# The first mixer's triangular inverse, merged in 32x32 tiles instead of full-width products

## Chip, cores and metric

One core of a Trainium2 chip runs the whole program. The metric is the device time of one execution in microseconds; three runs of the kernel before are shown.

## The reference, cut to what matters

The program is two layers of a sequence model on 2 x 2048 tokens of width 128: a gated delta-rule mixer, a two-deep windowed-attention block, a second (RWKV-like) mixer, another two-deep block, with norms between. Only the first mixer is touched. Per head (16 heads, keys of 64, values of 128) it is a recurrence over the tokens:

```
S = S * exp(g_t)
mem = k_t . S
delta = (v_t - mem) * b_t
S = S + k_t (x) delta
o_t = (q_t * scale) . S
```

The kernel does it in chunks of 128 tokens. Within a chunk the deltas solve a unit lower-triangular system per head: with A the decayed, scaled products of the chunk's keys, delta = (I + A)^-1 (v - decayed k.S), times beta. The change is in how (I + A)^-1 is built.

## The kernel before

The first mixer takes 32 chunks, one after the other (2 sequences of 16; a loop body of four chunks, run three times, and the last four written out). Sixteen heads go as four groups of four (`gi`), one PSUM bank a group. Every engine has its own order of work, written out by hand in its `body`; semaphores (`Signal`) tie them. While TensorE is in chunk n, the projections, decays and key products of chunks n + 1 and n + 2 are made ready between its steps.

The inverse has two parts. Ahead of the chunk, VectorE's `nA` (minus A, transposed; L824) is cut into its eight 16x16 diagonal blocks a head; they go through DRAM (`turn` on the DMA queue) so that VectorE's `inverse` works on all 128 blocks at once, and come back, transposed, as diagonal blocks of a zeroed `Tm`, [128, 16 heads, 128], which shares its buffer with `gV`. That landing is the signal `T_in`. Then `solve` on TensorE doubles the blocks three times (`LEVELS` 16, 32, 64). Before each level `turn_T` turns `Tm` (L496) and ScalarE copies it to `X` (L676). At a level, z = A times the even blocks (L512, for the last level L510), VectorE masks it into `Z` (L868), X times Z gives the block beside the diagonal (L521, last L519), and VectorE adds it to `Tm` (L876; last level: copies it into `X`, L873). Z keeps only the even blocks' 64 columns, but the weights, `X` or `Tm` and `nA`, are 128 rows by 128 columns, except in the last level. After it L531 applies `X` to the residues `R` (made by VectorE's `residues`, L860, from the state products L474), L537 and L543 make outputs and the new state.

Around it: `late` on ScalarE evicts the state's outputs (L671) before the first copy to `X`, and decays the state (L681) after the last. `X`'s buffer later holds squares and the turned output `yT`, read by L562, whose result VectorE takes in `tail`. POOL writes `gV` for the next chunk (`growth`, L984) once the last level's z is done, and zeroes `Tm` (L994) after masking the decays; `k_norms` (L977) runs in every second chunk. On VectorE the decays of the next chunk stand between the levels (`decays_first`, `decays_second`, L772 to L791).

## Time and profile before

| | |
|---|---|
| three runs, us | 5441.55, 5464.05, 5478.0 (median 5464.05) |
| profiled execution, span, us | 5452.6 |
| TensorE busy, us (share) | 4831.1 (89%) |
| VectorE busy, us (share) | 3836.5 (70%) |
| ScalarE busy, us (share) | 2736.9 (50%) |
| POOL busy, us (share) | 2285.8 (42%) |
| mean granted TensorE clock | 0.926 |

The span runs from the first to the last instruction of one execution; no time beside it was kept for that execution, so it stands among the three runs as one of its own. The engines overlap, so the shares don't add up. The granted clock is a share of 2.4 GHz. An fp32 matmul shows as two records, each with a weight load (PEld) and a product (PE); a turn shows as one.

### The profile page before, as it was taken

What the parts mean: (1) busy time and instruction counts of PE and PEld (TensorE: products, weight loads), DVE (VectorE), ACT (ScalarE), POOL (GpSimd) and SP (SyncE); (2) the same over time, 40 slices, a digit from 0 to 9 for tenths busy, and PEclk for the clock granted to TensorE, in tenths of its full rate; (3) what the DMA queues carried; (4) which work ended last, traced back from release to release, by engine and by line L of the source; (5) the groups of instructions that cost most, each with busy time, mean ns of one, the idle gap of its engine ahead of it and who ended that gap; (6) DMA issues with size and microseconds to landing.
All of it is one profiled execution on the core that took longest, in us unless ns stands there. A gap on an engine that the chain in (4) does not pass through costs nothing. (4 is left out here: it accounts for less than half of the span.)

```text
span 5452.6 us, 104905 instructions
## 1 busy us (share of the span) xinstructions
PE 4831.1 (89%) x36890; PEld 3535.1 (65%) x36890; DVE 3836.5 (70%) x9111; ACT 2736.9 (50%) x6711; POOL 2285.8 (42%) x1860
## 2 busy tenths in 40 slices
PE   5999999999999999999889989984488778998998
PEld 3787777877777787777766556641156665654665
DVE  4766667777677766767578668746699657866874
ACT  2444445444544544545478658724400116875882
POOL 2434334344334434434267347514322116743751
PEclk7999999999999999999999999986699758998998
DMA  2000000000000000000100000000000000000000
GB/s 86 5 9 7 7 9 7 7 9 7 7 9 10 5 9 8 6 9 9 34 1 0 25 5 0 0 7 0 8 1 1 1 1 30 0 24 5 0 0 16
DMA packets 170085, 52.60 MB, mean 10 GB/s; under 512 B 142304, under 2 KB 166112, under 8 KB 168928
## 3 DMA queue, kind: packets, MB, share of 16 engines
q1 hardware_dynamic: 168160, 44.30, 3.7%
q8 instruction: 232, 3.80, 0.3%
q10 hardware_dynamic: 1536, 3.21, 0.2%
q14 instruction: 157, 1.29, 0.1%
HBM read 36.99 MB, written 10.49 MB: 9 GB/s over the span
## 5 line engine op out<-in xcount | busy, mean ns | idle before, releaser
L799 DVE SCALAR_TENSOR_TENSOR gd_qkT<-gd_ps,gd_w_qk,gd_qkT 128x256 f32<-128x256 f32 x768 | 367.2, 482 | 193.3 <-ACT gd_qkT L632 172.7
L984 POOL TENSOR_TENSOR gd_gV<-gd_g,cst 128x512 f32<-128x512 f32 x128 | 130.3, 1040 | 860.1 <-PE gd_ps L510 860.1
L417 PE MATMUL gd_ps<-gd_taps,gd_xwins 128*128 128x512 f32 x1024 | 465.3, 597 | 0.0
L676 ACT ACTIVATE gd_X<-gd_ps 128x512 f32<-128x512 f32 x384 | 201.1, 620 | 452.9 <-PE gd_ps L496 452.6
L1540 ACT ACTIVATE L_ffn_s<-L_ffn_s,L_ffn_nb,L_ffn_r 128x128 f32<-128x128 f32 x1024 | 419.4, 482 | 3.1
L1360 POOL TENSOR_TENSOR L_ffn_t<-L_ffn_t 128x512 f32<-128x512 f32 x128 | 190.2, 1486 | 391.8 <-DVE L_ffn_t L1581 391.8
L417 PEld LDWEIGHTS gd_ps<-gd_taps,gd_xwins 128*128 128x128 f32 x1024 | 192.8, 191 | 191.1 <-issue 185.6
L868 DVE TENSOR_TENSOR gd_Z<-gd_ps,cst 128x256 f32<-128x256 f32 x384 | 162.7, 424 | 129.6 <-PE gd_ps L512 111.1
L1579 DVE TENSOR_TENSOR L_ffn_t<-L_ffn_ps,L_ffn_sb_rope 128x512 f32<-128x512 f32 x256 | 176.8, 691 | 101.8 <-PE L_ffn_ps L1385 101.8
L521 PE MATMUL gd_ps<-gd_Z,gd_X 128*128 128x64 f32 x2048 | 239.2, 275 | 0.0
L512 PE MATMUL gd_ps<-gd_gV,gd_nA 128*128 128x64 f32 x2048 | 237.9, 275 | 0.0
L512 PEld LDWEIGHTS gd_ps<-gd_gV,gd_nA 128*128 128x128 f32 x2048 | 236.3, 194 | 0.0
L521 PEld LDWEIGHTS gd_ps<-gd_Z,gd_X 128*128 128x128 f32 x2048 | 233.8, 192 | 0.0
L1428 PEld LDWEIGHTS L_ffn_ps<-L_ffn_kT,L_ffn_qT 64*64 64x64 f32 (+1 forms) x4096 | 148.5, 137 | 113.7 <-issue 98.2
L496 PE MATMUL gd_ps<-cst,gd_gV 128*128 128x128 f32 x1536 | 194.6, 280 | 31.0 <-DMA gd_gV<-gd_inverses 28.9
L860 DVE SCALAR_TENSOR_TENSOR gd_v<-gd_ps,gd_n_ec,gd_v 128x128 f32<-128x128 f32 x512 | 135.2, 342 | 123.0 <-PE gd_ps L474 120.8
L1362 POOL TENSOR_TENSOR L_ffn_r<-L_ffn_ss,L_ffn_mhalf 128x8 f32<-128x8 f32 x128 | 210.8, 1647 | 10.3 <-DVE L_ffn_ss L1603 5.1
L1029 POOL TENSOR_TENSOR gd_gate<-gd_gate,gd_o 128x512 f32<-128x512 f32 x128 | 159.5, 1277 | 126.3 <-DVE gd_o L885 126.3
L1369 POOL TENSOR_TENSOR L_ffn_r<-L_ffn_ss,L_ffn_mhalf 128x8 f32<-128x8 f32 x128 | 210.8, 1647 | 0.0
L990 POOL TENSOR_TENSOR gd_decay<-gd_decay,cst 128x512 f32<-128x512 f32 x128 | 186.7, 1490 | 47.1 <-ACT gd_decay L664 46.9
L687 ACT ACTIVATE gd_X<-gd_o 128x128 f32<-128x128 f32 x512 | 150.3, 295 | 106.0 <-DVE gd_o L885 106.0
L496 PEld LDWEIGHTS gd_ps<-cst,gd_gV 128*128 128x128 f32 x1536 | 175.3, 147 | 39.0 <-DMA gd_gV<-gd_inverses 32.2
(389 smaller groups left out, 13625.6 us busy)
## 6 DMA issues: line engine op xcount, KB each, us to landing
L_ffn_sb_rope<-in_rope SPq DMA_DIRECT2D x4, 2048.0 KB, 8.3
gd_tap_row<-in_L_attn_conv_v SPq DMA_DIRECT2D x2, 2048.0 KB, 15.6
gd_blocks<-gd_nA SPq DMA_DIRECT2D x256, 16.0 KB, 1.7
gd_Z<-gd_blocks SPq DMA_DIRECT2D x32, 128.0 KB, 2.0
gd_inverses<-gd_Z SPq DMA_DIRECT2D x32, 128.0 KB, 1.7
gd_gV<-gd_inverses SPq DMA_DIRECT2D x256, 16.0 KB, 1.9
L_ffn_sb_wqkv<-in_L_ffn_wqkv SPq DMA_DIRECT2D x4, 768.0 KB, 8.9
out<-out_tok SPq DMA_DIRECT2D x8, 256.0 KB, 2.6
```

Source lines behind the costliest of these rows:

```text
L417: ins = pe.matmul(ps[4 + i % 2][:], xwin(j)[:, t:t + P], taps[:, t, 512 * i:512 * (i + 1)], start=(t == 0), stop=(t == TAPS - 1))
L496: ins = pe.transpose(ps[4 + gi][:, P * k:P * (k + 1)], Tm[:, HG * gi + k], ident)
L512: ins = pe.matmul(ps[gi][:, 64 * k:64 * (k + 1)], nA[:, h], even(Tm, h, h + 1, s)[:, 0], start=True, stop=True)
L521: ins = pe.matmul(ps[gi][:, 64 * k:64 * (k + 1)], X[:, h], Z[:, h], start=True, stop=True)
L676: act.activation(heads(X, gi).rearrange("p h x -> p (h x)"), ps[4 + gi][:], ACT.Copy).then_inc(x_s.sem, 1)
L799: ins = dve.scalar_tensor_tensor(produced(j, i), ps[6 + i % 2][:, P + t:P + t + WIDE], w_tap[:, at, t:t + 1], produced(j, i), ALU.mult, AL ...
L990: pool.tensor_tensor(heads(decay, gi), heads(decay, gi), cst[:, C_UPTO:C_UPTO + P].unsqueeze(1).to_broadcast([P, HG, P]), ALU.mult).then_i ...
L1360: pool.tensor_tensor(t1[b][:, K], t1[b][:, K], t2[b][:, K], ALU.add).then_inc(la.k_sum.sem, 1)
L1362: pool.tensor_tensor(rk, ss[b][:, AH:2 * AH], mhalf[:, 0:AH], ALU.pow).then_inc(la.r_k.sem, 1)
L1369: pool.tensor_tensor(rq, ss[b][:, 0:AH], mhalf[:, 0:AH], ALU.pow).then_inc(la.r_q.sem, 1)
L1540: ins = act.activation(s[b][:, i, k], s[b][:, i, k], ACT.Exp, scale=r[b][:, h:h + 1], bias=nb[b][:, i, k:k + 1])
L1579: dve.tensor_tensor(a, xh, tb[0], ALU.mult)
```

## The change

The 16x16 blocks no longer go into a 128-wide zeroed matrix. `Tb` [128, 16, 32] keeps for each head the blocks of a 32-token quarter in that quarter's own 32 partitions, 16 columns a block; `Tt` is the same with each 32x32 square turned, made by VectorE's `transpose`. Three merges follow, each for two halves of eight heads in place of four groups of four:

- 16 to 32: `below_16` and `merged_32`, four 32x32 tiles of TensorE in the diagonal quarters (rows and columns `quad(r)`), 16 columns streaming. ScalarE evicts with a per-partition mask, VectorE adds into `Tb` and turns it again.
- 32 to 64: `below_32` and `merged_64`, 32x32 tiles, 32 columns streaming. The results go to `TL` (upper 64, ScalarE) and, turned, straight beside `X`'s diagonal (VectorE's `beside_32`).
- 64 to 128: `below_64` and `merged_128`, one 64x64 tile, 64 columns streaming; the block goes to `X`'s upper right (`upper_right`).

No full-width turns and no copies to `X` of all 128 columns remain; `X` is zeroed by POOL (`clear_X`, after the previous chunk's `tail`) and its diagonal filled by ScalarE from `Tt`. The waits on the state's outputs, on `Tm`'s levels and on `z` are replaced accordingly; `residues` is split into four calls among VectorE's new steps, and `decays_first` is moved ahead of them. The table of masks shrinks to one column. The rest of the program is unchanged.

```diff
-LEVELS = [16, 32, 64]
+BLOCK = 2 * BASE
...
+        Tb = gV_flat[:, 0:H * BLOCK].rearrange("p (h x) -> p h x", h=H)
+        TL = gV_flat[:, H * BLOCK:H * (BLOCK + HALF)].rearrange("p (h x) -> p h x", h=H)
+        Tt = gV_flat[:, H * (BLOCK + HALF):H * (2 * BLOCK + HALF)].rearrange("p (h x) -> p h x", h=H)
         PT, yT, y, squares = decay, X, delta, X
         qk_sq = delta[:].rearrange("p h x -> p (h x)").rearrange("p (i t) -> p i t", i=PAIRS)
...
+        Z16 = sysflat[:, 0:H * BASE].rearrange("p (h x) -> p h x", h=H)
+        Z32 = sysflat[:, 0:H * BLOCK].rearrange("p (h x) -> p h x", h=H)
...
+        def eight(t, i):
+            return t[:, H // 2 * i:H // 2 * (i + 1)]
+
+        def quad(r):
+            return slice(BLOCK * r, BLOCK * (r + 1))
+
+        def by_head(t, n):
+            return t[:, 0:H // 2 * n].rearrange("p (h x) -> p h x", h=H // 2)
...
-                        sp.dma_start(diagonal(Tm, q), inverse_dram[q].rearrange("h i j -> i h j")).then_inc(T_in.sem, 16)
+                        sp.dma_start(Tb[BASE * q:BASE * (q + 1), :, BASE * (q % 2):BASE * (q % 2 + 1)],
+                                     inverse_dram[q].rearrange("h i j -> i h j")).then_inc(T_in.sem, 16)
...
+                def below_16(i):
+                    for k in range(H // 2):
+                        h = H // 2 * i + k
+                        for r in range(4):
+                            ins = pe.matmul(ps[4 + i][quad(r), BASE * k:BASE * (k + 1)], nA[quad(r), h, quad(r)], Tb[quad(r), h, 0:BASE], start=True, stop=True)
+                    ins.then_inc(z16_mm.sem, 1)
+
+                def merged_32(i):
+                    for k in range(H // 2):
+                        h = H // 2 * i + k
+                        for r in range(4):
+                            ins = pe.matmul(ps[6 + i][quad(r), BASE * k:BASE * (k + 1)], Tt[quad(r), h], Z16[quad(r), h], start=True, stop=True)
+                    ins.then_inc(t16_mm.sem, 1)
+
+                def below_32(i):
+                    for k in range(H // 2):
+                        h = H // 2 * i + k
+                        for r in (1, 3):
+                            ins = pe.matmul(ps[4 + i][quad(r), BLOCK * k:BLOCK * (k + 1)], nA[quad(r - 1), h, quad(r)], Tb[quad(r - 1), h], start=True, stop=True)
+                    ins.then_inc(z32_mm.sem, 1)
+
+                def merged_64(i):
+                    for k in range(H // 2):
+                        h = H // 2 * i + k
+                        out = ps[6 + i][:, BLOCK * k:BLOCK * (k + 1)]
+                        pe.matmul(out[quad(1)], Tt[quad(1), h], Z32[quad(1), h], start=True, stop=True)
+                        for r in (3, 1):
+                            ins = pe.matmul(out[quad(r - 1)], Z32[quad(r), h], Tt[quad(r), h], start=True, stop=True)
+                    ins.then_inc(t32_mm.sem, 1)
+
+                def below_64(i):
+                    for k in range(H // 2):
+                        h = H // 2 * i + k
+                        ins = pe.matmul(ps[4 + i][HALF:P, HALF * k:HALF * (k + 1)], nA[0:HALF, h, HALF:P], TL[0:HALF, h], start=True, stop=True)
+                    ins.then_inc(z64_mm.sem, 1)
+
+                def merged_128(i):
+                    for k in range(H // 2):
+                        h = H // 2 * i + k
+                        ins = pe.matmul(ps[6 + i][0:HALF, HALF * k:HALF * (k + 1)], Z[HALF:P, h], X[HALF:P, h, HALF:P], start=True, stop=True)
+                    ins.then_inc(t64_mm.sem, 1)
 
                 def solve(n):
+                    def reached():
+                        pe.sem_inc(pe_reached, 1)
+
                     w(T_in.now(n))
+                    for i in range(2):
+                        w(o1_s.now(n, i))
+                        reached()
+                        below_16(i)
+                    for i in range(2):
+                        w(o1_s.now(n, 2 + i)); w(tt16_s.now(n, i)); w(z16_s.now(n, i))
+                        reached()
+                        merged_32(i)
+                    for i in range(2):
+                        w(T32_s.now(n, i))
+                        reached()
+                        below_32(i)
+                    for i in range(2):
+                        w(tt32_s.now(n, i)); w(z32_s.now(n, i))
+                        reached()
+                        merged_64(i)
+                    for i in range(2):
+                        w(TL_s.now(n, i))
+                        reached()
+                        below_64(i)
+                    for i in range(2):
+                        w(z64_s.now(n, i)); w(x32_s.now(n, i)); w(xd_s.now(n, 1))
+                        reached()
+                        merged_128(i)
                     for gi in range(G):
+                        w(R_s.now(n, gi)); w(X_s.now(n, gi // 2)); w(xd_s.now(n, 3))
                         for k in range(HG):
                             h = HG * gi + k
                             ins = pe.matmul(bank(gi)[:, k], X[:, h], R[:, h], start=True, stop=True)
...
-                    for l in range(NL):
-                        for gi in range(G):
-                            w(x_mm.now(n, G * l + gi))
-                            act.activation(heads(X, gi).rearrange("p h x -> p (h x)"), ps[4 + gi][:], ACT.Copy).then_inc(x_s.sem, 1)
+                    for i in range(2):
+                        w(z16_mm.now(n, i))
+                        act.activation(eight(Z16, i), by_head(ps[4 + i], BASE), ACT.Copy, scale=cst[:, C_MERGE:C_MERGE + 1]).then_inc(z16_s.sem, 1)
+                    for i in range(2):
+                        w(z32_mm.now(n, i))
+                        act.activation(eight(Z32, i), by_head(ps[4 + i], BLOCK), ACT.Copy).then_inc(z32_s.sem, 1)
+                    for r in range(2):
+                        act.activation(TL[quad(r), :, quad(r)], Tb[quad(r)], ACT.Copy)
+                    for i in range(2):
+                        w(t32_mm.now(n, i))
+                        act.activation(eight(TL, i)[quad(1), :, quad(0)], by_head(ps[6 + i], BLOCK)[quad(1)], ACT.Copy).then_inc(TL_s.sem, 1)
+                    w(X_zero.now(n)); w(tt32_s.now(n))
+                    for r in (2, 3):
+                        act.activation(X[quad(r), :, quad(r)], Tt[quad(r)], ACT.Copy).then_inc(xd_s.sem, 1)
+                    for i in range(2):
+                        w(z64_mm.now(n, i))
+                        act.activation(eight(Z, i)[HALF:P], by_head(ps[4 + i], HALF)[HALF:P], ACT.Copy).then_inc(z64_s.sem, 1)
+                    for r in (0, 1):
+                        act.activation(X[quad(r), :, quad(r)], Tt[quad(r)], ACT.Copy).then_inc(xd_s.sem, 1)
...
+                def residues(n, gi):
+                    w(nec_s.now(n)); w(ks_mm.now(n, gi)); w(vn_s.now(n, gi))
+                    for k in range(HG):
+                        h = HG * gi + k
+                        ins = dve.scalar_tensor_tensor(R[:, h], bank(gi)[:, k], n_ec[:, h:h + 1], v[:, h], ALU.mult, ALU.add)
+                    ins.then_inc(R_s.sem, 1)
+
+                def turn_16(n):
+                    w(T_in.now(n))
+                    for i in range(2):
+                        dve.transpose(eight(Tt, i), eight(Tb, i)).then_inc(tt16_s.sem, 1)
+
+                def blocks_32(n):
+                    for i in range(2):
+                        w(t16_mm.now(n, i))
+                        low = eight(Tb, i)[:, :, 0:BASE]
+                        dve.tensor_tensor(low, by_head(ps[6 + i], BASE), low, ALU.add).then_inc(T32_s.sem, 1)
+                        w(T32_s.now(n, i))
+                        dve.transpose(eight(Tt, i), eight(Tb, i)).then_inc(tt32_s.sem, 1)
+
+                def beside_32(n):
+                    w(X_zero.now(n))
+                    for i in range(2):
+                        w(t32_mm.now(n, i))
+                        dve.tensor_copy(eight(X, i)[quad(0), :, quad(1)], by_head(ps[6 + i], BLOCK)[quad(0)])
+                        dve.tensor_copy(eight(X, i)[quad(2), :, quad(3)], by_head(ps[6 + i], BLOCK)[quad(2)]).then_inc(x32_s.sem, 1)
+
+                def upper_right(n):
+                    for i in range(2):
+                        w(t64_mm.now(n, i))
+                        dve.tensor_copy(eight(X, i)[0:HALF, :, HALF:P], by_head(ps[6 + i], HALF)[0:HALF]).then_inc(X_s.sem, 1)
...
                 def body(n, b, c, j, s, follows, more):
                     if follows:
                         square_sums(n + 1, j + 1, s)
-                    residues(n)
-                    level(n, 0)
                     if follows:
                         decays_first(n + 1)
-                    level(n, 1)
+                    turn_16(n)
+                    residues(n, 0)
+                    residues(n, 1)
+                    blocks_32(n)
+                    residues(n, 2)
+                    residues(n, 3)
+                    beside_32(n)
                     if follows:
                         decays_second(n + 1, j + 1, s)
-                    level(n, 2)
+                    upper_right(n)
                     updates(n, j)
...
-                    pool.memset(Tm[:], 0.0).then_inc(Tm_zero.sem, 1)
+                    pool.memset(gV_flat[:, 0:H * (BLOCK + HALF)], 0.0).then_inc(Tm_zero.sem, 1)
...
+                def clear_X(n):
+                    w(out_s.before(n))
+                    pool.sem_inc(pool_reached, 1)
+                    pool.memset(X[:], 0.0).then_inc(X_zero.sem, 1)
...
+                    clear_X(n)
+                    if follows and j % 2 == 1:
+                        k_norms(n + 1)
                     if follows:
-                        if j % 2 == 1:
-                            k_norms(n + 1)
-                        w(g_s.now(n + 1)); w(z_mm.now(n))
+                        w(g_s.now(n + 1)); w(z64_mm.now(n)); w(xd_s.now(n))
                         growth(n + 1, 0)
```

## Rows read from the trace of the kernel before

**Rows 1.** the page: busy time of the engines, 40 slices, granted clock

```profile
PE 4831.1 (89%) x36890; PEld 3535.1 (65%) x36890; DVE 3836.5 (70%) x9111; ACT 2736.9 (50%) x6711; POOL 2285.8 (42%) x1860
...
PE   5999999999999999999889989984488778998998
...
PEclk7999999999999999999999999986699758998998
```

**Rows 2.** stretches: ahead of a solve, and the solve

```profile
1000.00:1052.90 52.90, 50.01 (x363) 36.09 (x361) 41.28 (x108) 27.93 (x86) 32.12 (x26) 1.00 0.07 11
...
1052.90:1076.20 23.30, 23.30 (x241) 23.07 (x241) 14.88 (x51) 9.16 (x23) 1.57 (x3) 1.00 0.01 2
```

**Rows 3.** waits of TensorE in the first mixer: us, times, longest

```profile
PE gd_ps L454 <- ACT gd_qkT L636: 45.6, 15, 3.0
...
PE gd_ps L496 <- DMA gd_gV<-gd_inverses: 26.9, 16, 2.8
```

**Rows 4.** timeline of TensorE in one solve: start, us, line, count, idle before

```profile
1047.62 2.06 PE L490 MATMUL gd_ps<-gd_S,gd_qkT 64*128 64x128 f32 x32 [0.69 <-ACT gd_gate L644]
...
1052.88 1.97 PE L496 MATMUL gd_ps<-cst,gd_gV 128*128 128x128 f32 x16 [1.42 <-DMA gd_gV<-gd_inverses]
...
1054.69 3.68 PE L512 MATMUL gd_ps<-gd_gV,gd_nA 128*128 128x64 f32 x32
...
1072.47 1.90 PE L510 MATMUL gd_ps<-gd_gV,gd_nA 128*64 128x64 f32 x29
...
1076.17 3.84 PE L531 MATMUL gd_ps<-gd_v,gd_X 128*128 128x128 f32 x32
```

**Rows 5.** timeline of ScalarE around the same solve

```profile
1046.97 0.60 ACT L644 ACTIVATE gd_gate<-gd_ps 128x512 f32<-128x512 f32 x1 [1.16 <-PE gd_ps L425]
...
1048.82 4.23 ACT L671 ACTIVATE gd_o<-gd_ps,gd_e_c 128x128 f32<-128x128 f32 x16 [1.25 <-PE gd_ps L490]
...
1053.58 2.06 ACT L676 ACTIVATE gd_X<-gd_ps 128x512 f32<-128x512 f32 x4 [0.53 <-PE gd_ps L496]
...
1073.19 5.16 ACT L681 ACTIVATE gd_S<-gd_S,gd_e_c 64x128 f32<-64x128 f32 x16
```

**Rows 6.** timeline of VectorE in the same solve

```profile
1050.66 4.22 DVE L860 SCALAR_TENSOR_TENSOR gd_v<-gd_ps,gd_n_ec,gd_v 128x128 f32<-128x128 f32 x16 [2.92 <-PE gd_ps L474]
...
1055.73 0.42 DVE L868 TENSOR_TENSOR gd_Z<-gd_ps,cst 128x256 f32<-128x256 f32 x1 [0.84 <-PE gd_ps L512]
...
1072.75 0.17 DVE L791 SCALAR_TENSOR_TENSOR gd_beta<-gd_tmp,gd_k_inv 128x16 f32<-128x16 f32 x1
...
1074.93 1.76 DVE L873 COPY gd_X<-gd_ps 64x256 f32<-64x256 f32 x4
```

**Rows 7.** timeline of TensorE, two column tiles in turn

```profile
2780.51 0.22 PE L1449 MATMUL L_ffn_ps<-L_ffn_vs,L_ffn_pT 128*64 128x65 f32 x1
2780.51 0.22 PE L1449 MATMUL L_ffn_ps<-L_ffn_v,L_ffn_pT 128*64 128x65 f32 x1
2780.56 0.22 PE L1449 MATMUL L_ffn_ps<-L_ffn_vs,L_ffn_pT 128*64 128x65 f32 x1
```

**Rows 8.** timeline of POOL

```profile
1019.55 1.81 POOL L994 MEMSET gd_gV<- 128x2048 f32 x1
```

**Rows 9.** stretches: engines' busy time, then granted clock

```profile
1114.20:1117.60 3.40, 3.18 (x30) 3.18 (x32) 2.94 (x12) 0.17 (x1) 1.04 (x1) 0.50 0.03 7
...
455.40:475.90 20.50, 18.97 (x84) 14.30 (x85) 0.19 (x1) 6.47 (x15) 1.24 (x3) 0.50 0.06 6
...
4312.50:4394.40 81.90, 68.43 (x399) 62.41 (x396) 34.70 (x19) 19.48 (x54) 18.45 (x4) 0.50 0.00 1
```

**Rows 10.** timeline of TensorE: L454 in two chunks

```profile
1032.55 2.06 PE L454 MATMUL gd_ps<-gd_qkT 64*128 64x128 f32 x32
...
1114.42 3.56 PE L454 MATMUL gd_ps<-gd_qkT 64*128 64x128 f32 x32 [3.05 <-ACT gd_qkT L636]
```

**Rows 11.** timeline of TensorE in the later mixer

```profile
4343.47 1.00 PE L2429 MATMUL wo_ps_s<-wo_S,wkv_vT 128*128 128x8 f32 x4
```

More of the change, by code:

```diff
@@ L299, in gated_delta @@
         inv_s, inv_out, T_in, Tm_zero = sig("inverse", 1), sig("inverse_out", 16), sig("T_in", 16 * NB), sig("T_zero", 1)
-        NL = len(LEVELS)
-        Tl_s = sig("T_level", G * NL)
-        z_mm, z_s, tz_mm = sig("z_mm", G * NL), sig("Z", G * NL), sig("tz_mm", G * NL)
-        x_mm, x_s = sig("x_mm", G * NL), sig("X", G * NL)
+        z16_mm, z16_s, t16_mm, T32_s = (sig(name, 2) for name in ("below_16_mm", "below_16", "merged_32_mm", "T_32"))
+        tt16_s, tt32_s = sig("T_16_turned", 2), sig("T_32_turned", 2)
+        z32_mm, z32_s, t32_mm, TL_s, x32_s = (sig(name, 2) for name in ("below_32_mm", "below_32", "merged_64_mm", "T_upper_64", "X_beside"))
+        z64_mm, z64_s, t64_mm, X_s = (sig(name, 2) for name in ("below_64_mm", "below_64", "merged_128_mm", "X"))
+        pe_reached, pool_reached = sems("gd_pe_reached"), sems("gd_pool_reached")
+        X_zero, xd_s = sig("X_zero", 1), sig("X_diagonal", 4)
         ks_mm, R_s = sig("ks_mm", G), sig("R", G)
@@ L331, in pair @@
             return (h // 8) * 4 + h % 4
-        def even(t, h0, h1, s):
-            return t[:, h0:h1].rearrange("p h (n two s) -> p h n two s", two=2, s=s)[:, :, :, 0, :]
+        def eight(t, i):
[4 more added lines that the diff above has]
+            return t[:, 0:H // 2 * n].rearrange("p (h x) -> p h x", h=H // 2)
         def diagonal(t, q):
@@ L492, in query_products @@
                                     ins.then_inc(qs_mm.sem, 1)
-                def turn_T(n, gi):
-                    for k in range(HG):
-                        ins = pe.transpose(ps[4 + gi][:, P * k:P * (k + 1)], Tm[:, HG * gi + k], ident)
-                    ins.then_inc(x_mm.sem, 1)
+                def below_16(i):
[4 more added lines that the diff above has]
+                    ins.then_inc(z16_mm.sem, 1)
@@ L527, in solve @@
-                    for gi in range(G):
-                        w(Tl_s.now(n, G * (NL - 1) + gi))
+                    for i in range(2):
[10 more added lines that the diff above has]
+                        below_32(i)
@@ L672, in late @@
                         ins.then_inc(o1_s.sem, 1)
-                    for l in range(NL):
-                        for gi in range(G):
-                            w(x_mm.now(n, G * l + gi))
-                            act.activation(heads(X, gi).rearrange("p h x -> p (h x)"), ps[4 + gi][:], ACT.Copy).then_inc(x_s.sem, 1)
+                    for i in range(2):
[17 more added lines that the diff above has]
+                        act.activation(X[quad(r), :, quad(r)], Tt[quad(r)], ACT.Copy).then_inc(xd_s.sem, 1)
                     for gi in range(G):
```

55 lines of the change are left out of this document (4 added, 51 removed).

## The prediction

> **What bounds the kernel now.** I read the page first, for the shares of the engines [rows 1]. TensorE is busy 89% of the span, VectorE 70%, the others about half. In the first 20 slices, which hold the first mixer, TensorE's digit is 9 almost throughout, and its granted clock 9 as well. So in the mixer TensorE's own order of work is the path, and a shorter order on TensorE is a shorter kernel as long as nobody else becomes late. Then the table by stretch [rows 2]: in one chunk the solve, from the first turn of `Tm` to the last merge, takes 23.3 us, TensorE is busy for all of it at the full clock (2.4 GHz), and VectorE (14.9) and ScalarE (9.2) are not. Then the waits of TensorE over the mixer [rows 3]: 45.6 us in 15 waits for ScalarE's last SiLU (L454), and 26.9 us in 16 waits for the inverse's DMA, together 73 of some 2,600 us. The solve is bound by its instructions, not by waits. Last the timeline of one solve [rows 4], which gives the pace. "x32" is 16 matmuls, since each fp32 product shows as two records. With a 128-column weight the records come every 110 ns (32 of L512 in 3.68 us, less the last one's 0.27) although only 64 columns stream; with a 64-column weight every 60 ns (29 of L510 in 1.90 us, less the last one's 0.22). So the width of the weight sets the pace, and a turn costs 113 ns (16 from 1052.88 to the next line's 1054.69).
>
> **What goes.** Per chunk 48 turns (5.4 us), 64 matmuls on 128-wide weights (14.1 us) and 32 on 64-wide ones (3.8 us): 23.3 us. With them go 12 ScalarE copies of `X` (3 x 2.06, [rows 5]) and, on VectorE, 12 masked copies, 8 sums and 4 copies of 0.42 to 0.44 us [rows 6].
>
> **What TensorE gets.** 64 + 64 + 32 + 48 = 208 matmuls on 32x32 tiles (416 records) and 32 on 64x64 tiles (64 records). The 64-wide ones keep L510's 60 ns: 0.96 us for a half of eight heads. No row shows a 32-wide tile. The upper bound is a lone 32-column weight at half of L510's pace, 30 ns, or 12.5 us for all. The lower bound is full overlap. Two 64-wide column tiles do overlap: L1449's two start together and the next one 50 ns later [rows 7], so the two share one tile's time. Four diagonal quarters in turn would then share 30 ns, 7.5 ns a record, 3.1 us in all. I take 14 ns, nearer to L1449, whose tiles overlap as these should; a half of 64 records is then 0.9 us. Between 7.5 and 14 the sum hardly moves, because the chain below is made of handoffs.
>
> **The chain of the new solve.** Only two halves, each step needing the one before, so latency counts. From a matmul's issue to ScalarE's start it is 0.7 us for four turns of 0.45 us, so 0.25 to 0.3 us of tail [rows 4, 5]; a wake of TensorE by ScalarE is 0.05 (the gate ends at 1047.57, L490 starts at 1047.62). Evictions: 128 columns 0.33 us (between L671's 0.26 pace and L676's 0.5), 256 columns 0.45, 512 columns 0.55. VectorE: 0.42 for 256 columns [rows 6], and I price a turn of 32x32 blocks, which no row shows, the same; at half or twice that price the end moves by nothing or by 1.5 us. From the landing of the inverse (T_in) in an even chunk, in us:
> VectorE turns both halves, 0.84, then does residues 0 and 1 (8 x 0.26), until 3.0; `below_16`, ScalarE, `merged_32` give half 0 at 3.0 too. Add and turn: T32 of half 0 at 3.4, second turned half at 4.8. `below_32` and ScalarE's copy: both halves at 5.7. `merged_64`: 6.1 and 6.9. ScalarE first fills two diagonal quarters of `TL` (2 x 0.5), then delivers it at 7.1 and 7.6. `below_64`: 8.4 and 9.4; ScalarE is at `X`'s lower diagonal until 8.7, then copies Z until 9.2 and 9.9. `merged_128`: 10.5 and 11.5 (0.3 of each the tail). VectorE (residues 2 and 3, the copies beside the diagonal, nine small decay operations of about 0.2 us [rows 6]) is free at 10.5, copies 0.6, and L531 starts at **11.2**. In an odd chunk the inverse lands early and `late` (16 x 0.26 us, [rows 5]) sets the first eviction, but the residues come earlier too; I count it the same. With 7.5 ns a record it is 10.9, with 30 ns 16.9.
>
> **What waits newly, and who stands behind it.** VectorE's first turn now waits for T_in with the residues behind it; their reader L531 comes 8 us after they end. ScalarE waits for the cleared `X` with Z's last copies and the decay of the state (5.16 us, [rows 5]) behind; that decay must end before the state's sum, which comes behind the whole of L531 (3.84 us [rows 4]), L537 and L543, and fits. The clearing on POOL costs about 1.8 us like the old memset of `gV` [rows 8], which itself shrinks by a quarter; it runs after the keys' decays, where POOL (42% busy) has time until `X` is first written, 7 us into the solve, and holds up only the key norms, which the next chunk wants. POOL's next growth now waits for `X`'s diagonal, so it starts with L531; its reader L466 stands behind L531, L537, L543 and a whole projection (L417) on TensorE. The eight DMAs of the inverse keep size and number. All cost nothing here; without that cover clearing would cost 1.8 us a chunk. The waits of [rows 3] stay: both begin behind the solve's end, and move with it.
>
> **What TensorE's clock does.** The old solve kept TensorE full. In the new one it streams 16 and 32 columns with holes between. After a hole of 3.05 us ahead of L454 the next stretch had half the clock (1.2 GHz) [rows 9] and L454 took 3.56 us instead of 2.06 [rows 10]. In the later mixer, 82 us with TensorE busy 84% of the time, largely by products of 8 columns (L2429 [rows 11]), stood at half clock throughout, and 20.5 us of this mixer at 93% did too [rows 9]. So I expect the clock to fall about halfway into the solve. The last two steps then take 1.9 instead of 0.96 us a half, and TensorE, now late at 14.8 by its own work, starts L531 at **14.8** in place of 11.2. After L531 dense work brings the clock back; L454's price for that was 1.5 us, I take **2.0** (1.5 to 3.5).
>
> **The sum.** 23.3 - 14.8 - 2.0 = 6.5 us a chunk, 32 chunks: 208 us. The profiled execution has a span of 5452.6 us, between the lowest and the median of the runs shown (5441.55 and 5464.05), so the sum gives 5245 for it and, 11.4 higher, 5256 as a median. About 1%, 55 us, is what a measurement of this kernel can tell from no change.
>
> **The rivals.**
> The clock holds (A): the solve ends at 11.2 and nothing is paid after, 12.1 x 32 = 387 us, 5077. For it: the page's clock digit in the mixer is 9 in nearly every slice, so falls there are short. Against: [rows 9, 11].
> Tiles don't overlap, or records are issued no faster than one per 30 ns (B): 16.9 us at the full clock, with nothing paid after, gives 205 us, 5259, the forecast's time by another way; with the clock fallen for the last two steps 20.2 + 2.0, a gain of 1.1 x 32 = 35 us, 5429. For it: no row shows a pace much faster than L1449's two in 50 ns. Against: that pace is what two 64-wide tiles need anyway. The Trainium skill, "TensorEngine Tiling (Array Packing)", section "Performance Considerations" (Instruction Overhead), speaks for B: each matmul has some 60 cycles of overhead, one free column costs as much as 60, and one should not tile a dimension that is already small. That is an estimate of 25 ns a record at 2.4 GHz and would make 10.4 us of the 416. No row here shows so small a tile; L1449's two starts at one time show that two tiles' starts need not keep that distance.
> Slower (C): no overlap, and half clock doubles each record: 416 x 60 ns + 64 x 120 ns = 32.6, plus 2.0 after: 11.3 us more than now, x 32 = 362 us, 5826. It decides from 33 ns a record on, with the 64-wide ones at 120 ns. For it: both halves of it have rows. Against: it needs both from the first microsecond.
> The gain is taken by a wait (D): if the inverse's DMA or the SiLU became the path, no change, 5464. Against: both chains start after L531 and shift with it.
>
> **How the numbers follow.** Forecast 0.45; A 0.20; B 0.10 at the full clock and 0.13 with it fallen; C 0.07; D 0.05. The range 5070 to 5430 leaves out C, D and about half of the slower B: 0.18. Faster by over 1% (below 5409): the forecast, A, the quicker B, and 0.05 of the slower B, which lies 20 us above that line, 0.80. Within 1%: the rest of it and D, 0.13. Slower: C, 0.07.
>
> **What the changed profile would show.** From the inverse's landing to L531's first record about 15 us instead of 23.3; quarters' records at under 15 ns in a burst; TensorE idle within the solve behind ScalarE and VectorE in turn, none of it over 2 us; granted clock at half in the later part of the solve and the first microseconds of L531; L531 to the next T_in as before plus some 2 us; waits at L454 and for T_in of the same sizes. Wrong it would be with records at 30 ns or more, a 32x32 turn on VectorE over 1 us, an eviction of 32 partitions slower than one of 128, or a clock that stays at half into the dense work after the solve.

## The result, and the profile after

The changed kernel takes 5315 us (5308 to 5321) where the kernel before takes 5459 on the same chip: a ratio of 0.973, 95% interval 0.970 to 0.977. The forecast was 5256, in a range of 5070 to 5430. The direction was right, and the gain is 144 us, or 4.5 us a chunk, where I had worked out 208 us, or 6.5. The profiled execution took 5314.12 us, its span is 5312.3 us against 5452.6, so the two traces carry the difference.

The page of the changed kernel; the lines answer to [rows 1]. The last is the queue that brings TensorE's instructions (queue, kind: packets, MB, share of 16 engines); the line of the kernel before stands below it by itself:

```profile
PE 4563.9 (86%) x44570; PEld 3259.9 (61%) x44570; DVE 3708.1 (70%) x8727; ACT 2767.1 (52%) x6775; POOL 2332.2 (44%) x1892
...
PE   5888988999898898989799899964588788998998
...
PEclk7888879888887898888799899977799659998998
...
q8 instruction: 292, 4.78, 0.4%
```

```profile
q8 instruction: 232, 3.80, 0.3%
```

TensorE has 267 us less to do, but only 140 us of the span are gone: in the first 20 slices its digits fell from 9 to 8 and 9, and its clock's from 9 to 8 and, in places, 7. It issues 7680 records more (240 a chunk, and as many weight loads). That is 480 instructions more a chunk, 15360 over the 32 chunks. The instruction queue brings 60 packets and 0.98 MB more than before, which is 64 bytes for each of them.

The timeline of TensorE in one even chunk, from the first step of the solve to the products behind it, answers to [rows 4] (start, us, line, count, idle before and what ended it). Chunks are counted from 0 here; the odd ones are then those in which the solve mostly waits for the inverse to land, which the prediction calls even.

```profile
1074.02 1.31 PE L511 MATMUL gd_ps<-gd_gV,gd_nA 32*32 32x16 f32 x128
1076.20 0.56 PE L518 MATMUL gd_ps<-gd_Z,gd_gV 32*32 32x16 f32 x47 [0.88 <-ACT gd_Z L726]
1078.58 1.06 PE L518 MATMUL gd_ps<-gd_Z,gd_gV 32*32 32x16 f32 x79 [1.82 <-issue]
...
1082.46 0.58 PE L525 MATMUL gd_ps<-gd_gV,gd_nA 32*32 32x32 f32 x14 [1.60 <-issue]
...
1085.30 3.36 PE L540 MATMUL gd_ps<-gd_gV,gd_nA 64*64 64x64 f32 x29 [0.51 <-ACT gd_gV L734]
...
1088.74 3.30 PE L546 MATMUL gd_ps<-gd_X,gd_Z 64*64 64x64 f32 x29
1091.97 5.92 PE L582 MATMUL gd_ps<-gd_v,gd_X 128*128 128x128 f32 x32
1097.73 2.51 PE L588 MATMUL gd_ps<-gd_delta,gd_decay 128*128 128x128 f32 x21
```

L511 is `below_16`, L518 `merged_32`, L525 `below_32`, L540 `below_64`, L546 `merged_128`, and L582 the product with the inverse that was L531. Three things are to be read here. The burst is fast: 128 records of L511 in 1.31 us less the last one's 0.2, so some 9 ns each, not far from the 7.5 of full overlap of the four quarters. Then TensorE stands still twice, 1.82 and 1.60 us, "issue": no engine, no DMA that the profile shows had to finish first. And the 64-wide steps and L582 take 3.3 and 5.9 us where [rows 4] had 60 ns a record and 3.84 us.

The table by stretch of the same chunk answers to [rows 2] (stretch, its us, busy time and instructions of TensorE, its weight loads, VectorE, ScalarE, POOL, then granted clock, DMA share, GB/s):

```profile
1074.02:1075.30 1.28, 1.28 (x130) 1.21 (x128) 1.28 (x6) 1.28 (x7) 0.00 (x0) 1.00 0.00 0
...
1078.58:1082.46 3.88, 2.28 (x126) 2.10 (x126) 3.42 (x12) 0.39 (x1) 0.00 (x0) 0.59 0.03 6
1082.46:1085.30 2.84, 2.33 (x115) 2.23 (x116) 1.34 (x4) 2.04 (x5) 0.00 (x0) 0.50 0.03 6
1085.30:1091.97 6.67, 6.67 (x65) 6.55 (x65) 2.57 (x11) 4.84 (x11) 0.88 (x1) 0.50 0.01 1
1091.97:1097.73 5.76, 5.76 (x33) 5.76 (x33) 2.76 (x4) 4.06 (x13) 3.39 (x5) 0.62 0.01 3
...
1074.02:1091.97 17.95, 13.15 (x483) 12.59 (x481) 8.76 (x32) 9.45 (x25) 0.88 (x1) 0.65 0.02 4
```

From one hole's end to the next (second row) TensorE took 126 products and 126 weight loads; with the few records that a trace can lack, that is 256 instructions. In this chunk the clock stands at 1.00 until some 0.7 us behind the first hole, 5.3 us into the solve, and from there at 0.50 (1.2 GHz) until 1096.3, three quarters of the way through L582. In the 32 chunks it falls between 0 and 5.6 us into the solve, 3.5 us on the mean. Averaged over the 32 chunks of the trace, from the first record of the solve to the first of L582: 23.7 us before, 17.5 after; L582 itself 3.84 and 5.77. That is 4.23 us a chunk, 135 of the 140 us.

The waits of TensorE in the first mixer, which answer to [rows 3] (us, times, longest), here with those that "issue" ended:

```profile
PE gd_ps L518 <- issue: 53.8, 36, 2.5
PE gd_ps L467 <- ACT gd_qkT L687: 45.7, 15, 3.1
...
PE gd_ps L525 <- issue: 31.8, 17, 2.4
...
PE gd_ps L511 <- DMA gd_gV<-gd_inverses: 20.2, 14, 2.7
PE gd_ps L534 <- issue: 20.2, 17, 1.9
...
PE gd_ps L532 <- issue: 10.0, 9, 1.5
...
PE gd_ps L511 <- issue: 1.2, 2, 0.7
```

The two old waits (L467 was L454, L511 stands where L496 stood) have not grown. New are 117 us of "issue" inside the solve (53.8 + 31.8 + 20.2 + 10.0 + 1.2), in 81 waits, 3.66 us a chunk. In the trace of before, one line of the first mixer waits for "issue":

```profile
PE gd_ps L431 <- issue: 11.6, 6, 2.7
```

None of these six is in a solve: they stand behind the jumps of the loop, L431 being the first line of its body. The changed kernel has them as well (L444, 11.8 us).

What brings the instructions is seen in the view of the DMA queues, here from 1075 to 1087 us in 40 slices of 0.3 us:

```profile
GB/s 0 0 0 55 0 0 0 0 0 0 0 0 0 0 0 0 55 0 0 0 0 27 0 0 0 0 0 0 0 55 0 0 0 0 0 0 0 0 0 0
...
q8 instruction: 3, 0.05, 1.7%
```

Three packets of 16 KB (0.05 MB in 3), in slices 3, 16 and 29 from 0 on, so 3.9 us apart; TensorE goes on some 2.5 us behind the start of the first (at 1078.58) and of the second (at 1082.46). At 64 bytes, 16 KB are 256 instructions. The pattern holds in the whole trace: ahead of each of the 81 waits' ends a packet starts 2.2 to 3.0 us earlier, and of the 49 waits that follow another in the same solve 47 end 252 or 254 records of products and weight loads behind it. Within the solves packets start 3.3 to 4.7 us apart, 3.8 on the mean. The six waits of before have a packet 2.5 to 3.0 us ahead of their end, too.

So two theories stood for the missing 64 us. **Supply**: TensorE's instructions come in blocks of 256, and a block that is worked off in less than some 3.9 us leaves it without instructions for the rest. **Clock**: with holes and small tiles the clock is at half for most of the solve and into L582. The rival of the first: the holes are handoffs between engines that the profile doesn't show, and only pace counts.

### The profile page after: what moved, and what is told of

Read it like the earlier page. It is cut to its first block and busy times, and to the rows that moved or that the text cites. A ratio compares the mean times of both kernels' runs of the same rounds, so it can differ in the third digit from the quotient of the medians.

```text
span 5312.3 us, 119470 instructions
## 1 busy us (share of the span) xinstructions
PE 4563.9 (86%) x44570; PEld 3259.9 (61%) x44570; DVE 3708.1 (70%) x8727; ACT 2767.1 (52%) x6775; POOL 2332.2 (44%) x1892
## 5 line engine op out<-in xcount | busy, mean ns | idle before, releaser
L430 PEld LDWEIGHTS gd_ps<-gd_taps,gd_xwins 128*128 128x128 f32 x1024 | 192.4, 191 | 190.9 <-issue 185.4
L1512 PEld LDWEIGHTS L_ffn_ps<-L_ffn_kT,L_ffn_qT 64*64 64x64 f32 (+1 forms) x4096 | 148.5, 137 | 114.2 <-issue 98.7
L1512 PE MATMUL L_ffn_ps<-L_ffn_kT,L_ffn_qT 64*64 64x128 f32 (+1 forms) x4096 | 195.3, 280 | 0.0
L1059 POOL TENSOR_TENSOR gd_v<-gd_v,gd_k_norm 128x512 f32<-128x512 f32 x128 | 131.9, 1042 | 144.4 <-ACT gd_v L691 144.4
L2315 POOL TENSOR_TENSOR wkv_S<-wkv_S,ws_vk 128x512 f32<-128x512 f32 x64 | 80.3, 1277 | 258.9 <-DVE ws_vk L2383 258.9
L1523 PEld LDWEIGHTS L_ffn_ps<-cst,L_ffn_s 128*128 128x128 f32 x1024 | 107.3, 140 | 135.2 <-ACT L_ffn_s L1624 68.0
L582 PE MATMUL gd_ps<-gd_v,gd_X 128*128 128x128 f32 x1024 | 184.8, 363 | 0.0
L582 PEld LDWEIGHTS gd_ps<-gd_v,gd_X 128*128 128x128 f32 x1024 | 178.7, 275 | 3.8
L1523 PE MATMUL L_ffn_ps<-cst,L_ffn_s 128*128 128x128 f32 x1024 | 167.6, 286 | 12.6 <-ACT L_ffn_s L1624 9.4
L683 ACT ACTIVATE gd_qkT<-gd_ps,gd_w_qk 128x256 f32<-128x256 f32 x256 | 120.2, 474 | 111.7 <-PE gd_ps L410 111.7
```

Source lines behind the costliest of these rows:

```text
L430: ins = pe.matmul(ps[4 + i % 2][:], xwin(j)[:, t:t + P], taps[:, t, 512 * i:512 * (i + 1)], start=(t == 0), stop=(t == TAPS - 1))
L582: ins = pe.matmul(bank(gi)[:, k], X[:, h], R[:, h], start=True, stop=True)
L1512: ins = pe.matmul(ps_s[i][rows, P * k:P * (k + 1)], qT[b][half(i), k, rows], kT[b][half(i), k, WIN * wd:WIN * wd + P], start=True, stop=True)
L1523: ins = pe.transpose(ps_p[i][:, P * k:P * (k + 1)], s[b][:, i, k], ident)
```

## The experiments

In all of them the first mixer alone is changed. They stand in the order in which they ran.

**1. Twice the 16-products** (`e1_double16`).

```
-                    for k in range(H // 2):
+                    for k in [k for k in range(H // 2) for again in range(2)]:
```

> Every product of the two 16-merges below the diagonal (L511, 128 records a chunk) is issued twice in a row; the second writes the same values again. Supply theory: TensorE's holes in the solve come every 256 records of weight loads and products, and a block of 256 takes about 3.9 us to be supplied; 128 more products are 256 more records, one more block in the solve: +3.0 to +3.9 us a chunk, 5410 to 5440 us, and the solve shows one hole more. Rival (pace and waits only: the holes are handoffs between engines that the profile doesn't show): 128 records at the 8.5 to 10 ns measured, +1.1 to +1.3 us a chunk, 5350 to 5357 us, with the holes where they were.

Measured: 5436 us, 0.996 (0.995 to 0.998) of the kernel before, so 121 us or 3.8 us a chunk above the changed kernel, as the supply theory had it. The waits of TensorE and the page's line on the queue:

```profile
PE gd_ps L518 <- issue: 70.6, 35, 2.6
PE gd_ps L511 <- issue: 63.6, 35, 2.6
...
PE gd_ps L525 <- issue: 27.3, 17, 2.1
PE gd_ps L534 <- issue: 21.4, 17, 1.7
...
PE gd_ps L532 <- issue: 10.0, 9, 1.4
```

```profile
q8 instruction: 323, 5.29, 0.4%
```

193 us of holes instead of 117, 113 waits instead of 81 (one a chunk more), 31 packets more. The 128 added records a chunk bring 256 instructions and cost what a block costs; at their burst's pace they would have cost 1.1 us. They take away five sixths of the change's gain.

**2. Half of the 16-merges left out** (`e2_half16`; the same edit in L511 and in L518).

```
-                        for r in range(4):
+                        for r in (2 * (k % 2), 2 * (k % 2) + 1):
```

> Leaves out half of the 32-tile products of the 16-merges (two of the four quarters of each head, the upper pair for one head and the lower for the next, in L511 and in L518): 128 products a chunk fewer, with every other engine's work and all waits as they were; the inverse is not computed in the quarters left out. Supply theory: one block of 256 records fewer in the solve, so one of the two holes goes: -1.8 to -3.9 us a chunk, 5190 to 5255 us. Rival (pace and waits only): two bursts of 1.3 us become 0.65 us, of which about 1 us lies on the path: -0.7 to -1.2 us a chunk, 5277 to 5293 us, and two holes stay.

Measured: 5218 us, ratio 0.956 (0.953 to 0.958), 98 us or 3.05 us a chunk below the changed kernel and again where the supply theory had it. The same two views, and the bounds of the 64-wide steps in chunk 13, which has no hole:

```profile
PE gd_ps L534 <- issue: 20.9, 14, 2.3
...
PE gd_ps L532 <- issue: 12.7, 9, 2.4
PE gd_ps L525 <- issue: 7.8, 10, 1.5
PE gd_ps L518 <- issue: 4.2, 3, 2.0
```

```profile
q8 instruction: 260, 4.26, 0.3%
```

```profile
1107.65 0.72 PE L511 MATMUL gd_ps<-gd_gV,gd_nA 32*32 32x16 f32 x64 [1.83 <-DMA gd_gV<-gd_inverses]
...
1114.78 3.32 PE L540 MATMUL gd_ps<-gd_gV,gd_nA 64*64 64x64 f32 x29 [0.51 <-ACT gd_gV L734]
...
1121.39 5.69 PE L582 MATMUL gd_ps<-gd_v,gd_X 128*128 128x128 f32 x32
```

45.6 us of holes are left and 32 packets are gone, one a chunk. The two runs on either side of the changed kernel settle the first theory: the same 256 instructions a chunk are worth 121 us upwards and 98 downwards, and pace alone allowed 42 and 38 at most. They also show that the waits for instructions alone are not what brings the clock down: in the four chunks of this run without any hole it fell within the first 3.0 us of the solve, and the 64-wide steps take 3.66 us each, as in the changed kernel.

**3. Dense products between the steps** (`e3_dense`).

```
+                def dense(times):
+                    for t in range(times):
+                        pe.matmul(ps[0][:], ident, w_g[:, 0:512], start=True, stop=True)
...
+                    w(R_s.now(n, 0))
+                    dense(1)            # behind below_16; 2 behind merged_32, 2 behind below_32,
+                                        # 1 behind merged_64, 1 behind below_64
```

> Adds seven full products of 128x128 on 128x512 (0.87 us each at full clock) to the solve, between its steps: one after the first step, two after the second, two after the third, one after the fourth, one after the fifth. Their results are overwritten and nothing waits for them. Clock theory: the 64-wide steps (3.3 us for 32 records) and the products after the solve (5.8 us) are long because TensorE's clock is granted at half; with dense work between the steps it stays up, L540 and L546 take 1.9 us each and L582 3.8 us. Together with the supply theory, by which the holes of 3.6 us a chunk are filled by the added products and not added to: +6.1 -2.8 -1.9 -2 to -3.6 us, that is -0.6 to -2.2 us a chunk, 5245 to 5296 us. If the clock stays at half, the added products take 1.73 us each and the time goes up by 6 to 9 us a chunk (5510 to 5600 us). If the 64-wide steps are long for another reason, their durations stay at 3.3 us with the clock at 1.0, and the time is about 5360 us.

Measured: 5314 us, ratio 0.975 (0.973 to 0.977): the changed kernel's time, above the 5245 to 5296 expected. First the table by stretch, the solve in an even chunk, and two lines of TensorE's timeline in it; then groups of lines over the whole span (busy us, mean ns of one, idle before), where L551 are the added products and L592 stands for L582:

```profile
1070.08:1088.41 18.33, 16.27 (x496) 10.99 (x494) 8.77 (x32) 9.54 (x25) 0.88 (x1) 1.00 0.01 4
```

```profile
1071.62 1.13 PE L551 MATMUL gd_ps<-gd_w_g,cst 128*128 128x512 f32 x2
1072.68 1.35 PE L518 MATMUL gd_ps<-gd_Z,gd_gV 32*32 32x16 f32 x116
```

```profile
L551 PE MATMUL gd_ps<-gd_w_g,cst 128*128 128x512 f32 x448 | 284.7, 747 | 9.2 <-ACT gd_Z L736 4.7 <-DVE gd_v L934 2.5 <-issue 1.9
...
L592 PE MATMUL gd_ps<-gd_v,gd_X 128*128 128x128 f32 x1024 | 122.8, 279 | 0.0
...
L540 PE MATMUL gd_ps<-gd_gV,gd_nA 64*64 64x64 f32 x1024 | 66.4, 220 | 0.0
```

and the same two groups of the changed kernel:

```profile
L582 PE MATMUL gd_ps<-gd_v,gd_X 128*128 128x128 f32 x1024 | 184.8, 363 | 0.0
...
L540 PE MATMUL gd_ps<-gd_gV,gd_nA 64*64 64x64 f32 x1024 | 117.2, 312 | 5.1 <-ACT gd_gV L734 5.1
```

The clock theory is shown in its mechanism: with the clock at 1.00 a 64-wide step takes 2.08 us instead of 3.66 (66.4 and 117.2 over 32 chunks), and the product with the inverse is back at 3.84. (Over the whole solve the clock is 0.88 on the mean of the 32 chunks; in the 64-wide steps it is up in all of them.) The holes shrank, too (the largest group from 53.8 us to 26.5, the others to 3 in all), as would follow if the dense products pass the time in which the next block comes. But the bill was wrong: the added products took 8.9 us a chunk (284.7 over 32), not 6.1. Some of them, in the odd chunks mostly the first three, ran at half clock; and even at full clock one that stands alone among small tiles takes 1.06 us until the next line begins (1071.62 to 1072.68), not 0.87. Solve and product together are 23.1 us a chunk (19.24 + 3.84) where the changed kernel has 23.3.

**4. The gate projections moved into the solve** (`e4_gates`): useful dense work in the place of the idle one.

```
-                    w(gate_out.now(n, 3)); w(S_s.before(n))     # query_products
+                    w(tk_out.now(n, 1)); w(S_s.before(n))
...
                         below_16(i)
+                    project_gate(n, j, 0)                       # waits for R_s(n, i), writes ps[i]
+                    project_gate(n, j, 1)
...
                         merged_64(i)
+                    project_gate(n, j, 2)
+                    project_gate(n, j, 3)
```

> Moves the four gate projections (0.87 us each on TensorE, L438) with their Silus from ahead of the solve into it, two after the first step and two after the fourth, into the banks that the residues have left; the first two residues go ahead of VectorE's turn of the 16-blocks. Supply and clock theories: the projections lie where TensorE waits for instructions or for other engines, and raise the clock; in chunks where the inverse has landed early the stretch before the solve is 3 to 3.5 us shorter, in the others it isn't (the landing sets the start), and the solve grows by 0 to 1.5 us in both, while the products after it get 0 to 1.9 us back: -0.5 to -2.5 us a chunk on the mean, 5235 to 5300 us. Rival (the holes aren't filled, the clock stays): the solve grows by 3.5 us in both kinds of chunk, which the shorter stretch before it gives back in half of them: +0.5 to +1.8 us a chunk, 5331 to 5373 us.

Measured: 5294 us, ratio 0.970 (0.968 to 0.971), 21 us below the changed kernel (0.970 against 0.973 of the kernel before, with intervals that just meet), at the upper end of what supply and clock had. Where the rest went, in groups of lines of this kernel and then of the changed one:

```profile
L500 PE MATMUL gd_ps<-gd_S,gd_qkT 64*128 64x128 f32 x1024 | 119.1, 410 | 50.1 <-DVE gd_k_ss L880 38.7 <-DVE gd_q_eps L884 6.3 <-DVE x1T L985 4.4
L484 PE MATMUL gd_ps<-gd_S,gd_qkT 64*128 64x128 f32 x1024 | 89.8, 345 | 0.0
...
L583 PE MATMUL gd_ps<-gd_v,gd_X 128*128 128x128 f32 x1024 | 134.6, 295 | 35.9 <-ACT gd_X L746 35.2
```

```profile
L503 PE MATMUL gd_ps<-gd_S,gd_qkT 64*128 64x128 f32 x1024 | 71.3, 292 | 26.0 <-ACT gd_gate L695 22.0 <-DVE gd_q_eps L882 3.3 <-DVE x1T L983 0.7
...
L487 PE MATMUL gd_ps<-gd_S,gd_qkT 64*128 64x128 f32 x1024 | 64.3, 277 | 0.0
```

L583 came down to 134.6, but the query and state products ahead of the solve went from 135.6 us to 208.9: with the gates gone, the square sums (L418, products of two columns) stand alone in front of them, and now it is there that the clock falls: over the query products it is 0.50 to 0.62 in 30 of the 32 chunks, where the changed kernel has 0.98 or more in 29. In the odd chunks the shorter stretch ended in a wait for VectorE (38.7), and two Silus held up `X`'s diagonal for L583 (35.2). The half clock had been moved, not removed.

**5 to 7. Less dense work** (`f1_gates_split`, `f3_dense_few`, `f4_gates_dense`). The first leaves two gates ahead of the solve and spreads the other two over it in halves; the second is experiment 3 with three products; the third is the first with two added products.

```
+                    gate_half(n, j, 2, 0)       # behind below_16, 256 columns into ps[0]
+                    gate_half(n, j, 2, 1)       # behind merged_32
+                    gate_half(n, j, 3, 0)       # behind below_32, into ps[2]; + dense(1) in the third
+                    gate_half(n, j, 3, 1)       # behind merged_64;            + dense(1) in the third
```

> Leaves the first two gate projections ahead of the solve and moves the last two into it as four halves (0.44 us each at full clock), one behind each of the first four steps, into the banks that residues 0 and 2 have left; residue 0 goes ahead of VectorE's turn. The stretch ahead of the solve is 2.4 us shorter (two products of 0.87 us and the wait of 0.69 us for the last Silu), which counts where the inverse has landed early; the 1.7 us of products lie in the holes of the supply. Clock theory, if four halves hold the clock up: the 64-wide steps and L582's counterpart give 3 to 4.3 us back, -3.5 to -5 us a chunk, 5155 to 5205 us. If they don't hold it: -0.3 to -1.2 us a chunk, 5277 to 5305 us, with 64-wide steps of 3.3 us.

> The added full products of the dense experiment, but three a chunk in place of seven: one behind the second, third and fourth step. If these hold the clock up, the 64-wide steps take 2.1 us and L582's counterpart 3.84 us, and of the 2.6 us added some 1.9 us lie in the holes: -2.5 to -3.7 us a chunk, 5195 to 5235 us. If they don't, the steps stay at 3.3 and 5.8 us and the added products come on top: 0 to +2 us a chunk, 5315 to 5380 us.

> The split gates of the first of these three kernels, with two added full products whose result is overwritten, one behind the third step and one behind the fourth. Supply and clock theories: 1.7 us more of TensorE work than with the split gates alone, of which 0.5 to 1.5 us lies in a hole; the clock holds where four halves alone may not: -2.5 to -4.5 us a chunk against the changed kernel, 5170 to 5235 us. If the clock falls all the same: 5310 to 5350 us.

Measured: 5323 us, ratio 0.975 (0.972 to 0.979); 5430 us, 0.993 (0.990 to 0.996); 5287 us, 0.967 (0.964 to 0.970). The first two lie above all that was expected, the third between its two ranges, so none of the three came out as forecast. The group of the 64-wide step in each, and for the second the added products:

```profile
L548 PE MATMUL gd_ps<-gd_gV,gd_nA 64*64 64x64 f32 x1024 | 117.6, 313 | 0.0
```

```profile
L551 PE MATMUL gd_ps<-gd_w_g,cst 128*128 128x512 f32 x192 | 190.9, 1097 | 0.0
...
L540 PE MATMUL gd_ps<-gd_gV,gd_nA 64*64 64x64 f32 x1024 | 116.0, 310 | 0.0
```

```profile
L548 PE MATMUL gd_ps<-gd_gV,gd_nA 64*64 64x64 f32 x1024 | 71.9, 229 | 0.0
```

Neither four halves nor three whole products held the clock; then they run at half clock themselves and come on top (190.9 us, 6.0 a chunk, for three products, 2.0 us each). Halves and two whole ones held it in most chunks: 71.9. My reckoning had priced added work at the full clock even where the clock then fell; it costs double there.

**8 and 9. Another order ahead of the solve** (`g1_even`, `g2_late`), to cure what experiment 4 had shown. Both have the split gates and two or three added products in the solve.

```
g1_even:  sums 0, half gate, sums 1, half gate, sums 2, half gate, sums 3, half gate
g2_late:  sums 0, sums 1, whole gate, sums 2, half gate, sums 3, half gate; one dense(1) more behind merged_32
```

> The split gates with two added products, and ahead of the solve each of the four pairs of square sums (L418, products of 2 columns) is followed by half a gate projection (256 columns), so that no two of them stand back to back. In the run before, the two pairs that stood back to back were followed by the query and state products at a lower clock, 5.7 us a chunk for both in place of 4.2. Clock theory: these come back to about 4.1 us, 1.4 us a chunk less, of which the chunks that wait for the inverse's landing see little: 0 to -1.4 us a chunk against that run, 5240 to 5287 us. If the half projections don't hold the clock: 5285 to 5300 us, with the products at 5.7 us or more.

> As the kernel before it in this call, but ahead of the solve two square sums stand first, right behind the dense products of the output, then a whole gate projection, and only the last two are each followed by half a one; and a third added product stands in the solve, behind its second step. Clock theory: the added product (0.87 us, some of it in a hole) keeps the clock up in the chunks in which it fell with two; ahead of the solve 4.1 us for the query and state products, if the order holds the clock: 5225 to 5285 us. If neither helps: 5290 to 5315 us.

Measured: 5297 us, ratio 0.971 (0.968 to 0.975), and 5279 us, 0.968 (0.965 to 0.971). Half gates between the sums didn't hold the clock: the query and state products took 6.0 us a chunk in the first (109.7 + 83.4 over 32), 5.3 in the second (98.7 + 70.9), not the 4.1 expected: the first is in the range of its miss, the second in its range for part of the reason given. With the third added product the group of the 64-wide step took 66.7 us, where experiment 7 had 71.9.

**10 to 12. The best version beside the changed kernel, and its dense work alone** (`h1_dense_same`, `h2_after`, `h3_late`) on one chip. The second is the changed kernel and the third `g2_late`, once more; the first has all gates where the changed kernel has them, and in the solve added products of the same columns in the same places.

```
+                    dense(256)           # behind below_16
+                    dense(256, 512)      # behind merged_32, below_32 and merged_64
```

> All four gate projections stay ahead of the solve as in the changed kernel; the solve gets added products only, in the columns and places in which the kernel with the late gates has gate halves and added products (256, 256 and 512, 256 and 512, 256 and 512 columns behind the first four steps), overwritten later; residue 0 goes ahead of the turn. Clock theory: the solve and the products after it take what they take there, 18.7 and 3.8 us in place of 17.5 and 5.8, -0.8 us a chunk against the changed kernel: 5280 to 5300 us. What the kernel with the late gates has below that is the shorter stretch ahead of the solve. If only the gates' move counts: 5305 to 5325 us.

> The changed kernel once more, to stand beside the other two on one chip: 5300 to 5325 us, 0.973 of the kernel before.

> The kernel with the late gates and three added products once more: 0.968 of the kernel before, 30 to 40 us below the changed kernel on the same chip.

Measured: 5318 us, ratio 0.974 (0.973 to 0.976); 5304 us, 0.973 (0.971 to 0.975); 5282 us, 0.969 (0.967 to 0.971). The first missed its 5280 to 5300 and lies where it was to lie if only the gates' move counted: solve and product took 19.7 + 3.8 us a chunk, 0.2 to 0.3 more than the changed kernel. Dense work for the clock's sake alone gives back about what it costs, here and in experiment 3, and no more. The version with the late gates is 21 us quicker than the changed kernel, not the 30 to 40 expected, and the slowest of its five runs (5301) is slower than the fastest of the other's (5294). Its solve and product take 19.2 + 3.8 us, what the changed kernel's take, so its gain lies ahead of the solve, where two of the four gates are gone: part of the dense work in its solve had to be done anyway. The order of the square sums differs between these kernels as well, so this reading is argued and not isolated by a run.

## Why the prediction came out as it did

**What bounds the kernel** held. TensorE's own order was the path, and the time went where its order got shorter; neither wait of [rows 3] grew, so rival D is out.

**What TensorE gets: the lower bound was true, and harmless it was not.** In the bursts over four tiles records come 9 ns apart instead of my 14. Over two tiles, 45 records of `below_32` took 1.03 us at full clock in a chunk of experiment 2, some 18 ns each. Both are below the 30 ns of no overlap, so that half of B and the whole of C are refuted. The Trainium skill's rule ("TensorEngine Tiling (Array Packing)", "Instruction Overhead"), from which I had estimated 25 ns a record, doesn't bound a burst over four tiles: 9 ns.

**The step that failed is the solve's term, 14.8 us.** It priced each instruction by how long it streams and said that between 7.5 and 14 ns "the sum hardly moves". The sum lacks a wait: a faster burst only waits longer for the next 256 instructions. In the long run 3.8 to 3.9 us a block are 15 ns an instruction, 30 ns a record with its weight load. Rival B had that very number, as a steady pace with 12.5 us for all records; it came as bursts and holes. What was left of the solve's time beside the holes is close to the sum: 17.5 less 3.66 is 13.9 us. Where the holes are away, the handoffs come out as I had laid them: in the four chunks of experiment 2 without a hole, with halved bursts, the 64-wide steps begin 7.1 us behind the first record (`TL` was due at 7.1), and the 64-wide steps with their handoffs take 6.6 us (1114.78 to 1121.39). The holes were not in the sum, and no solve of before could have shown them, as its records took 60 to 110 ns each. But the trace of before had TensorE without instructions for up to 2.7 us behind the loop's jumps, and the count was there to be read from the diff, 480 records a chunk in the new solve. That the time still fell within the range is in part luck: the bursts were quicker than priced, which made up for some of the holes.

**The clock** fell as forecast, only earlier: 3.5 us into the solve on the mean and not halfway, in the chunk shown 5.3 us in, behind the first hole. Its price behind the solve was 1.93 us a chunk (5.77 for 3.84) where I had 2.0. In the 64-wide steps it was 1.6 us each (3.66 for 2.08), where I had 1.9 for a pair of halves. Rival A (the clock holds, 5077) failed twice: the clock fell, and its 11.2 us lack the holes. What the solve would take at full clock without added work no run shows; experiment 3 has the clock at 1.00 through the solve of the chunk shown and took 18.3 us there, with the products that hold it.

**The rest of the list.** VectorE's turn of 32x32 blocks takes 0.45 us a half (0.42 priced). ScalarE's eviction of 32 partitions and 256 columns takes 0.32 us, that of 128 partitions 0.39, so it isn't the slower one. POOL's clearing takes 1.80 us, ahead of the solve, as priced. The idle time behind ScalarE and VectorE in the solve stayed under 2 us; that behind the instructions, which wasn't on the list, didn't.

In sum, a chunk: 6.5 forecast; the solve gave 6.16 (23.7 less 17.5) instead of 8.5 (23.3 less 14.8), of which the holes of 3.66 took more than the whole difference of 2.3 and quicker bursts gave some back; L582's 1.93 for 2.0. That makes 4.23 us, 135 us of the 140 in the traces.

## What to carry to other kernels

Cutting a product into small tiles trades time on the array for instructions: count them, and ask of each stretch whether it has more of them than the rate at which they come, here 256 in some 3.8 us, allows. The stretch of small tiles cost the clock here, with holes and without, and the dense work behind it paid as well. Dense work that has to be done anyway is what to put there, but the gain was small, and where that work was taken from, the clock may fall instead. A rival that has the right number for the wrong picture is worth a second look before its chance is set low.

## What the hardware showed that I had not expected

TensorE runs out of instructions. Blocks of 16 KB come 3.3 to 4.7 us apart in the solves, 3.8 on the mean, and 256 instructions more or less a chunk move the time by 3.8 and 3.05 us. The Trainium skill, "Runtime: NRT & Kernel Launch", section "Instruction fetch mechanics", has the same block (16 KiB, 256 instructions, the next fetched while the current one runs) and calls the cost of a boundary mostly hidden. The trace agrees with the block and not with the rest: over the 32 solves it is 117 us. What makes up the 3.9 us of a block was not tried; the traces show when a packet starts and when TensorE goes on, some 2.4 us later, not who waits for whom in between.

What stands in front of dense work showed in its clock. The product with the inverse took 5.77 us behind the solve of the changed kernel and 3.84 behind that of experiment 3, where the clock over the solves was 0.60 and 0.88 on the mean. Three added products did not lift it (0.60 over the solves), and each of them took 2.0 us. And the query and state products, 135.6 us in the changed kernel, took 208.9 where the square sums of two columns stood alone ahead of them.
